# Thirty-six instead of thirty-two batches multiplied by the weight while x is first read, in a graph-layer kernel of Strassen products

## The reference, cut to what matters

```python
h = relu(layernorm(x))                  # x: 64 batches x 128 steps x 1024 nodes, float32
x_avg = mean of h over batches          # 1024 nodes x 128
sim = cosine similarity of the nodes    # 1024 x 1024, from x_avg
adj = (sim_score + gumbel0 > 1 - sim_score + gumbel1)
adj_sym = clip(adj + adj.T, 0, 1);  nmask = clip(adj_sym + eye, 0, 1)
common = nmask @ nmask.T
struct = where(adj_sym > 0 and common > 1, common / common.max() * common, 0)
W = adj * struct;  Wn = dinv[:, None] * W * dinv[None, :]
out = Wn.T applied to (h @ weight) over the nodes, for every batch, + bias
return x + out
```

## Time and profile before

| | |
|---|---|
| median of three runs | 921.62 us |
| the profiled execution, its own time | 921.26 us |
| its span | 919.5 us |
| TensorE busy | 887.7 us, 97% of the span |
| VectorE busy | 725.3 us, 79% |
| ScalarE busy | 328.0 us, 36% |
| GpSimd busy | 239.8 us, 26% |
| granted TensorE clock | 0.999 of full speed |

### The profile page before, as it was taken

The page is one execution under the profiler, slowest core; times in us unless marked ns, Lnnn a source line. Parts: engine busy times, 40 slices in busy tenths (PEclk is TensorE's granted clock), DMA queues, the critical chain, the costliest instruction groups (busy, mean ns, idle before and its releaser), DMA issues.

```text
span 919.5 us, 12305 instructions
## 1 busy us (share of the span) xinstructions
PE 887.7 (97%) x4563; PEld 761.4 (83%) x4567; DVE 725.3 (79%) x1471; ACT 328.0 (36%) x531; POOL 239.8 (26%) x188
## 2 busy tenths in 40 slices
PE   4999999999999999999999999999999999999997
PEld 3777665788788888888888888888889888988886
DVE  7878858899989797888879787868576758677687
ACT  4999935651221121302121211323333342424130
POOL 4799960500212121111111111302011111111111
PEclk9999999999999999999999999999999999999999
DMA  9999889233436170716344352615233252524122
GB/s 355 382 419 381 328 326 422 81 123 116 137 138 206 69 275 6 269 61 214 105 170 140 135 190 85 225 50 198 77 134 141 90 185 69 183 92 161 46 92 92
DMA packets 37484, 160.25 MB, mean 174 GB/s; under 512 B 3376, under 2 KB 3504, under 8 KB 32176
## 3 DMA queue, kind: packets, MB, share of 16 engines
q1 hardware_dynamic: 37424, 159.46, 46.8%
HBM read 108.07 MB, written 51.38 MB: 173 GB/s over the span
## 4 chain that ended last, share of the span: by engine, by line
PE 79%; DVE 9%; ACT 6%; POOL 3%; issue 2%; DMA 0%; DVEq 0%; ACTq 0%; POOLq 0%
PE ps L1354 69%; PE ps L1303 4%; ACT main L532 4%; DVE bmem L957 3%; POOL main L473 3%; ACT bmem L541 2%; PE ps L1224 2%; DVE stats L750 2%; PE ps L1206 1%; DVE bmem L950 1%; PE ps L1137 1%; PE ps L1284 1%; DVE main L1070 1%; DVE main L1046 1%; DVE bmem L969 0%
## 5 line engine op out<-in xcount | busy, mean ns | idle before, releaser
L1354 PE MATMUL ps<-bmem,main 128*128 128x256 f32 x3136 | 685.1, 379 | 4.0 <-DVE main L1037 2.6
L1354 PEld LDWEIGHTS ps<-bmem,main 128*128 128x128 f32 x3136 | 592.4, 190 | 83.3 <-DVE main L1037 3.5
L500 POOL TENSOR_TENSOR main<-main 128x256 f32<-128x256 f32 x32 | 28.7, 896 | 477.3 <-ACT main L659 424.0
L1037 DVE TENSOR_TENSOR main<-ps,main 128x512 f32<-128x512 f32 x124 | 76.5, 623 | 71.0 <-PE ps L1354 71.0
L490 POOL TENSOR_TENSOR main<-main 128x256 f32<-128x256 f32 (+1 forms) x96 | 91.9, 984 | 139.0 <-DVE main L1030 139.0
L1046 DVE TENSOR_TENSOR main<-main 128x256 f32<-128x256 f32 (+1 forms) x256 | 124.5, 558 | 0.0
L473 POOL TENSOR_TENSOR main<-main 128x1024 f32<-128x1024 f32 x41 | 96.9, 2364 | 23.4 <-ACT main L532 18.5
L619 ACT ACTIVATE ps<-ps 128x512 f32<-128x512 f32 x64 | 33.8, 528 | 159.2 <-PE ps L1354 159.2
L750 DVE BATCH_NORM_STATS2 stats<-main 128x6 f32<-128x512 f32 x128 | 81.2, 674 | 4.5 <-DMA main<-in_x 4.5
L877 DVE TENSOR_TENSOR main<-main 128x256 f32<-128x256 f32 x112 | 48.2, 431 | 44.7 <-PE ps L1354 41.5
L1137 PEld LDWEIGHTS ps<-w_sb,main 128*128 128x128 f32 x560 | 67.0, 194 | 15.0 <-issue 12.0
(11 more groups left out here) (101 smaller groups left out, 541.2 us busy)
## 6 DMA issues: line engine op xcount, KB each, us to landing
main<-in_x SPq DMA_DIRECT2D x92, 512.0 KB, 7.2
main<-in_x SPq DMA_DIRECT2D x32, 1024.0 KB, 6.7
out<-main SPq DMA_DIRECT2D x31, 1024.0 KB, 4.9
main<-spill SPq DMA_DIRECT2D x17, 1024.0 KB, 5.3
spill<-bmem SPq DMA_DIRECT2D x16, 1024.0 KB, 11.9
main<-in_L_gnn_gumbel SPq DMA_DIRECT2D x8, 1024.0 KB, 6.3
spill<-main SPq DMA_DIRECT2D x2, 512.0 KB, 4.6
out<-main SPq DMA_DIRECT2D x1, 512.0 KB, 4.9
```

What stands on the lines that cost most here:

```text
L1037: dve.tensor_tensor(at, piece(slot, b), at, ALU.add).then_inc(s, 1)
L1354: last = pe.matmul(piece(slot, b)[:, QUARTER * e:QUARTER * (e + 1)], left_[:, blk(c)], right_[:, c, :], start=slot in FRESH and b < 3 and ...
```

## The change

1. `SPILLED` gets two more pairs, 12 and 20: 18 pairs, 36 batches, are multiplied by the weight in stage 1. `LOADED` is then quads 2 to 10, `WEIGHED` quads 1 and 11 to 15, `EXTRA` is 11. Stage 3 multiplies four batches less.
2. `BOTH` has ten pairs in place of nine, other ones: GpSimd adds one batch more, TensorE one less.
3. The copies (5, 1), (9, 1), (13, 1) and (19, 1) are made by VectorE, before its last statistics instruction of groups 6, 8, 10 and 13. The other copies with b = 1 stand one step later in ScalarE's list: step p now makes the copy (p-4, 1) where it made (p-3, 1); the copy (p-2, 0) stays.
4. Six stores (twelve batches) stand between the reads of x in place of four, from p = 14 on.
5. Stage 2: of the first two transposed blocks, the parts that need only the first seven rows of `adj` stand ahead of the wait for the last.
6. The first quad of stage 3: slots 0, 2 and 6 issue first what needs only finished operands; VectorE adds up slot 4's results ahead of `prepare(6)` and makes the operands of quad 1's slot 0 earlier; `finish_kept(0, 1)` moves from quad 0 into quad 1.

```diff
-    SPILLED = [0, 1, 2, 3, 5, 7, 8, 9, 11, 13, 15, 17, 19, 21, 23, 26]
+    SPILLED = [0, 1, 2, 3, 5, 7, 8, 9, 11, 12, 13, 15, 17, 19, 20, 21, 23, 26]
-    SPILLED_EARLY = [15, 17, 19, 21]
-    HOMES = [*range(8, 16), *range(16, 24), *range(8), *range(8, 16)]
+    SPILLED_EARLY = [14, 16, 18, 20, 22, 24]
+    HOMES = [*range(8, 24), *range(8), *range(8, 20)]
+    BY_VECTOR = [5, 9, 13, 19]
+    LAG = (2, 4)
+    def product(p, b):
+        return 2 * SPILLED.index(p) + b
+    MADE = [product(q, b) for p in range(PAIRS) for q, b in ((p - 1, 1), (p, 0)) if q in SPILLED]
+    VECTOR_COPIES = [*(product(p, 1) for p in BY_VECTOR), KEPT - 2, KEPT - 1]
+    SCALAR_COPIES = [product(q, b) for p in range(PAIRS) for q, b in ((p - LAG[1], 1), (p - LAG[0], 0))
+                     if q in SPILLED and product(q, b) not in VECTOR_COPIES]
-    BOTH = [4, 6, 8, 11, 14, 16, 18, 20, 23]
+    BOTH = [4, 6, 8, 10, 12, 14, 16, 18, 20, 22]
+        def wait_copied(eng, n):
+            if n in VECTOR_COPIES:
+                eng.wait_ge(s_kept_vector, VECTOR_COPIES.index(n) + 1)
+            else:
+                eng.wait_ge(s_kept, SCALAR_COPIES.index(n) + 1)
+        def wait_made(eng, n):
+            eng.wait_ge(s_hw, MADE.index(n) + 1)
...
                 if p - HPAIRS in SPILLED:
-                    act.wait_ge(s_hw, 2 * SPILLED.index(p - HPAIRS) + 2)
+                    wait_made(act, product(p - HPAIRS, 1))
...
-                    if p - 3 in SPILLED[:-1]:
-                        keep(p - 3, 1)
-                    if p - 2 in SPILLED[:-1]:
-                        keep(p - 2, 0)
+                    for b in (1, 0):
+                        q = p - LAG[b]
+                        if q in SPILLED and product(q, b) in SCALAR_COPIES:
+                            keep(q, b)
...
+            def keep(p, b):
+                n = product(p, b)
+                wait_made(dve, n)
+                if HOMES[n] in HOMES[0:n]:
+                    dve.wait_ge(s_spill[HOMES.index(HOMES[n]) // 2], 16)
+                dve.tensor_copy(kept[:, HOMES[n], :], bank(2 + 2 * b, 2)).then_inc(s_kept_vector, 1)
...
                     long_step(t, 6)
+                    for p in BY_VECTOR:
+                        if t == (p + 7) // 2:
+                            keep(p, 1)
                     long_step(t, 7).then_inc(s_bn, 1)
...
             def keep_product(p, b):
-                n = 2 * SPILLED.index(p) + b
-                wait(pe, s_kept, n - 1)
+                n = product(p, b)
+                if n >= 2:
+                    wait_copied(pe, n - 2)
                 times_weight(h1[:, p % HPAIRS, b, :], 2 + 2 * b).then_inc(s_hw, 1)
...
-            transposes(0)
-            transposes(1)
+            for i in range(2):
+                for j in range(C - 1):
+                    transpose(i, j)
+            pe.wait_ge(s_adj, C)
+            for i in range(2):
+                transpose(i, C - 1).then_inc(s_tr, 1)
...
+                if quad == 1:
+                    inner_sums(quad, 3)
+                    finish_kept(0, 0, u_keep, s_g21, 0)
+                    finish_kept(0, 1, v_keep, s_g22, 8)
...
+                    if quad == 0 and slot in (0, 2, 6):
+                        if slot == 0:
+                            pe.wait_ge(s_comb, 4 * n + 4)
+                            pe.wait_ge(s_scaled, KC)
+                            pe.wait_ge(s_repc, 1)
+                            times(0, 0, 2, 0, q[0, 1], moving[1, 0])
+                            times(0, 0, 2, 1, s4, moving[1, 1])
+                            free(0, 0, 0)
+                            times(0, 0, 0, 0, q[0, 0], moving[0, 0])
+                            pe.wait_ge(s_repc, 2)
```

More of the change, by code:

```diff
@@ L338, in spill_group @@
             def spill_group(g):
[L339 to L342, removed]
+                wait_copied(sp, 2 * g)
+                wait_copied(sp, 2 * g + 1)
                 at = HOMES[2 * g]
@@ L678, in _ @@
                 for b in range(4):
-                    keep_bank(quad, 2, b, u_keep, 16 * quad, s_ukeep)
+                    keep_bank(quad, 2, b, u_keep, 8 if quad == 1 else 16 * quad, s_ukeep)
                     weigh(quad, (2, b))
                 for b in range(4):
-                    keep_bank(quad, 3, b, v_keep, 16 * quad - 8, s_vkeep)
+                    keep_bank(quad, 3, b, v_keep, 16 if quad == 1 else 16 * quad - 8, s_vkeep)
                     weigh(quad, (3, b))
@@ L768, in _ @@
                     for b in range(2):
[L769 to L772, removed]
+                        keep(SPILLED[-1], b)
                     whole_chain(t)
@@ L1008, in prepare @@
                     minus(rows_of(T4_ROWS), rows_of(B21_ROWS), rows_of(T2_ROWS), start)
+                    made_at["T4"] = made[0]
                     inner_of(6)
@@ L1094, in _ @@
                     inner_sums(quad, 2)
-                    finish_kept(quad - 1, 0, u_keep, s_g21, 16 * quad - 8)
                 else:
                     prepare(3)
-                if quad:
+                if quad == 1:
+                    inner_sums(quad, 3)
+                    finish_kept(0, 0, u_keep, s_g21, 0)
+                    finish_kept(0, 1, v_keep, s_g22, 8)
+                elif quad:
+                    finish_kept(quad - 1, 0, u_keep, s_g21, 16 * quad - 8)
                     inner_sums(quad, 3)
@@ L1109, in _ @@
                 if quad == 0:
+                    add_kept(quad, 4, v_keep, s_vkeep, s_g22)
                     prepare(6)
@@ L1113, in _ @@
                     finish_kept(quad, 0, u_keep, s_ukeep, 16 * quad)
-                add_kept(quad, 4, v_keep, s_vkeep, s_g22)
+                if quad:
+                    add_kept(quad, 4, v_keep, s_vkeep, s_g22)
                 if quad + 1 < QUADS:
@@ L1117, in _ @@
                 if quad == 0:
-                    finish(quad, 1)
-                    add_kept(quad, 6, u_keep, s_ukeep, s_g21, range(2))
-                finish_kept(quad, 1, v_keep, s_g22, 16 * quad + (0 if quad + 1 < QUADS else 8))
-                if quad:
-                    finish(quad, 1)
+                    add_kept(quad, 6, u_keep, s_ukeep, s_g21, range(1))
+                else:
+                    finish_kept(quad, 1, v_keep, s_g22, 16 * quad + (0 if quad + 1 < QUADS else 8))
+                finish(quad, 1)
                 if quad + 1 < QUADS:
-                    add_kept(quad, 6, u_keep, s_ukeep, s_g21, range(4) if quad else range(2, 4))
+                    add_kept(quad, 6, u_keep, s_ukeep, s_g21, range(4) if quad else range(1, 4))
                     dve.wait_ge(s_g21, 4 * quad + 4)
@@ L1209, in _, with transpose @@
             late_half(3, 1).then_inc(s_late_hw, 1)
-            pe.wait_ge(s_adj, C)
+            pe.wait_ge(s_adj, C - 1)
+            def transpose(i, j):
+                return pe.transpose(ps[:, 4 + i % 2, :].bitcast(BF16)[:, blk(j)], adj[:, j, blk(i)], identb[:, :])
             def transposes(i):
-                if i >= 2:
-                    pe.wait_ge(s_sym, i - 1)
+                pe.wait_ge(s_sym, i - 1)
                 for j in range(C):
-                    last = pe.transpose(ps[:, 4 + i % 2, :].bitcast(BF16)[:, blk(j)], adj[:, j, blk(i)], identb[:, :])
+                    last = transpose(i, j)
                 last.then_inc(s_tr, 1)
```

48 lines of the change are left out of this document (28 added, 20 removed).

## The result

The changed kernel takes 957.29 us (median of 4 runs, 956.19 to 958.29), the kernel before 922.25 (4 runs, 921.16 to 922.99): a ratio of 1.0381, 95% interval 1.0361 to 1.0400. It is slower by 35 us. The forecast was 937.2 us and its range ended at 942: the sign and the place were right, the size was less than half of what came.

The account below looks back on a forecast made before the run. TensorE was taken to bound stage 3 and ScalarE stage 1. Stage 1 +26.5, stage 3 -7.1, first quad and transposes -3.5 gave +15.9 on 921.26: 937.2 us, range 926 to 942.

Parts of the forecast that it names:

- the chunks': Stage 3: eight chunks of matmuls fewer, 0.89 us each on the chain; gain 7.1 us.
- the order of waits: Stage 1, the deciding term: later ScalarE copies with b = 1 make engines wait; stage 1's end +26.5 us.
- The ring: Inside one ScalarE step of stage 1, copy, product, product, copy wait in turn; 4.85 us where ScalarE needs 0.90.
- The count by engine: Stage 1: each engine's added work, leaving out who waits for whom; growth of 1.6 to 5.4 us.
- (a): GpSimd's adds keep the end of stage 1; only the extra add shows, +1.6 us, 912.3 us in all; chance 0.08.
- (b): TensorE sets the pace of stage 1; +5.4 us, 916.1 us in all; chance 0.05.
- (c): Stage 1: only the full rings cost, +12.4 to +19 us, 923 to 930 us in all; chance 0.10.
- Rival (d): Stage 1: VectorE waits for products, so statistics are late; another 5 to 10 us, 942 to 947 us; chance 0.07.
- the three handoffs: Stage 1: copy to waiting product 1.08 us, product to next product 1.79, product to waiting copy 1.98; sum 4.85.
- full gap: ScalarE's wait in stage 1 between copies (p-4, 1) and (p-2, 0); forecast 3.95 us, four times.
- half gap: ScalarE's wait in stage 1 between copy (p-4, 1) and relu(p+1); forecast 2.16 us, four times.
- the walk: Step-by-step count of stage 1's in-order lists and measured handoffs; its end at 149.7, +26.5 us; chance 0.70.

Follow-up runs that it names:

- experiment 1: Changed kernel with ScalarE's copies with b = 1 back at step p-3 (LAG = (2, 3)); 916.02 us, ratio 0.9935.
- Experiment 8: experiment 5 with `finish_kept(0, 1)` moved behind the operands of slot 4 in quad 1; 912.46 us, ratio 0.9900.
- experiment 5: experiment 1 with, in quad 1, `finish_kept(0, 0)` ahead of slot 3's operands and `finish_kept(0, 1)` behind `finish(1, 0)`; 913.82 us, ratio 0.9907.
- 6: Experiment 3 with quad 1's VectorE order as in experiment 5; 920.53 us, ratio 0.998.
- Experiment 2: Changed kernel with 12 or 19 unused 128x128 products ahead of each of the eight products that close a ring; 943.93 us, ratio 1.0243.
- experiment 7: experiment 1 with VectorE's four copies back on ScalarE (`BY_VECTOR` empty); 918.06 us, ratio 0.9951.
- Experiment 3: Changed kernel with stage 1's lists as before (32 batches) and LAG = (2, 3), only transposes and quads changed; 922.26 us, ratio 0.9999.
- experiment 4: Experiment 3 with ScalarE's copies with b = 1 one step later (LAG = (2, 4)); 944.31 us, ratio 1.0244.

## Why the prediction was wrong in size and right in mechanism

**The ledger in spans.** Forecast: +26.5 - 7.1 - 3.5 = +15.9. Measured: stage 1 +40.8, its end +2.5, transposes and quad 0 -3.7, quad 1 +4.5 (experiment 1 against 8), and with the chunks' -7.1 (experiment 5 against 6) that is +37.0 of the +37.1.

**Right: the order of waits.** The ring is there, in the steps that were named, and it alone costs (experiment 1). The count by engine, which the prediction worked out and then did not believe (+1.6 to +5.4 us), came out as +1.8 once the ring was opened: the count is good as long as nobody waits, and says nothing of a ring. Rivals (a), (b) and (c) are out, for the gaps are all there and larger. Rival (d) had VectorE's statistics late behind its copies. Its 942 to 947 us come nearest of all, but its mechanism is not what happened: ScalarE's waits for VectorE in stage 1 after 20 us are 1.2 + 0.2 us.

**The step that failed: the price of the three handoffs.** The prediction took 1.79 us for a product and 1.98 from a product's start to the copy behind it, both from the earlier trace rows, where TensorE had idled 1.25 us or less and ran at 1.00. No sentence of it asked for the clock behind the waits that it forecast, so the lower level stood in the sum at nothing, without a reason. The first handoff holds, 27.96 to 29.02 is 1.06 (1.08). From the product at 29.02 to the copy at 34.52 it is 5.50, where 1.79 + 1.98 = 3.77 were taken. In starts, a full gap is 34.52 - 27.96 = 6.56 three times (44.46 and 75.51 alike) and 99.48 - 94.54 = 4.94 once, against 4.85; a half gap is 52.67 - 47.64 = 5.03 three times and 4.40 once, against 1.08 + 1.98 = 3.06.

- full gaps: 3 x 6.56 + 4.94 - 4 x 4.85 = +5.2 us
- half gaps: 3 x 5.03 + 4.40 - 4 x 3.06 = +7.3 us
- small waits, step 23 and what else the rows leave over: 14.3 - 12.5 = +1.8 us, not taken apart

Together they are the 14.3 us by which stage 1 (164.05 - 149.7) was missed. Experiment 2 takes the clock's share away and leaves 151.40 - 149.7 = 1.7 of it. So 12.65 of the 14.3 us (164.05 - 151.40) hang on the clock, and the walk's own logic was off by 1.7 us over 27 us.

The Trainium skill (TensorE: Matmul & The Clock Gate, Part 1: The HAM clock gate) says that the halved rate is TensorE's default state and that activity releases the full one, with nothing in between; the rows show these two levels (0.50 at 30 to 32 us, 1.00 at 34 to 36). The same page (Why this matters for your kernels) advises against idle gaps between bursts of matmuls, above a length that it names. The rule spoke against this change and was not weighed. Taken by its length alone it would still have missed the turns at 38.95 and 70.01 us, where the clock fell behind gaps of 2.75 us, which are shorter; the rows decide. A forecast of waits on TensorE has to ask what its first work behind each wait costs at the lower level: here 3.55 us (48.79 to 52.34) for one product that takes 1.79, and 5.47 for two that take 3.73.

**Not foreseen: the end of stage 1, +2.5 us.** "It moves as a block" supposed that VectorE's L853 is the last thing to be late. With the ring TensorE is late too, and its column sums come 3.95 us behind L853 in place of 1.4. In experiment 1 the same L857 follows L853 without that wait (125.01 to 128.49); in experiment 7 it waits 1.16 us. From L853 to the first matmul of stage 3 the distance is 229.00 - 164.05 = 64.95 us against 187.55 - 123.21 = 64.34 before, within the 1 us that the forecast allowed; that is luck, since the 2.5 us are offset by the wait of 1.39 us that is gone and by smaller gains.

**Right: the first quad.** TensorE's idle time there goes from 1.39 + 0.48 + 1.76 + 0.89 = 4.5 us to 0.61 + 0.49 = 1.1: 3.4 us. The transposes give 0.3. Forecast 3.5, measured 3.7. The row that the prediction held against this part did not decide it: the eight moved sums and the eight beside them take 7.05 us together in quad 1, 0.44 each, though the operands L908, L911 and L914 took 0.95, 0.94 and 0.83 us from 274.30 on, beside GpSimd's adds.

**Wrong: the quad that receives `finish_kept`.** The prediction found 42.00 - 34.69 = 7.3 us of VectorE free there and cost the move at nothing. Free time on average is not free time at the place: the piece of 7.05 us stands ahead of `finish(1, 0)`. Experiment 8, which differs from experiment 1 in the places of this piece's two halves alone, is shorter by 915.1 - 910.6 = 4.5 us. Of these 2.5 are the wait, and most of the rest is the clock behind it. In medians it is 916.02 - 912.46 = 3.6: two of experiment 1's four executions had spans of 913.4 and 913.5 and a clock of 0.999, where the profiled one had 0.997. In experiment 2 the same wait of 2.48 us was not followed by a lower clock, and the stretch from its end to the end of the span took 942.2 - 286.24 = 655.96 us there, against 956.6 - 298.92 = 657.68 in the changed kernel: 1.7 us is the clock's share. Experiment 3 shows the balance, 3.7 won and some 4.5 lost, and no change in the time that can be measured. So the forecast's -3.5 for the order of the first quads was right for quad 0 and came to nothing as a whole.

**Right: stage 3.** L1345 has 384 records, and experiments 5 and 6 differ by 7.1 us from quad 1 on, for 36 batches against 32.

**What stays open.** Which idle stretches lower the clock can't be told from these runs: 2.75 us did at 36 to 39 us and did not at 93 to 96, and some 2.5 us in quad 1 did in the changed kernel and did not in experiment 2. Even one kernel differs: of experiment 3's ten executions eight had a span of 920.4 us or more and a mean clock of 0.997 or less, and two had 918.9 and 0.999. That these two are the ones without the fall in quad 1 fits the 1.7 us, but was not seen in a profile, and the kernel before, which has no such wait in quad 1, falls into two groups as well: beside experiment 3, six of its thirteen executions had a span of 920.0 us or less and seven 921.1 or more, with a clock of 0.997 or less. In experiment 4 a wait of 2.75 us at 73 us was not followed by a fall, and the first full gap came to 6.59 us. A forecast can only hold both ends.

## What to carry to other kernels

When two in-order engines hand buffers to each other, write down for each instruction who frees its buffer, and follow the chain until it comes back to the same engine. If it returns inside one step, every handoff is paid at each turn, and no count of busy time shows it. Price each handoff with the durations that TensorE has after an idle stretch of that length, not with those from a stretch in which it never idled; keep both as ends of the range. And before a piece of work is put where an engine is free on average, look at what stands right behind it in that engine's list and who waits for that.

## What the runs showed of the hardware

Unexpected was that the lower clock hit nearly every turn of the ring. TensorE's idle stretches of 2.75 to 4.37 us were followed by the 1.2 GHz level in seven of the eight turns of rings, while from 23 to 123 us it was busy for 73.76 of 100 us. Filling these stretches with 124 matmuls of 128x128 of no use won 14.4 us of span (956.6 - 942.2). One product (16 records) right behind a stretch of 4.37 us took some 3.6 us, where it takes 1.79 otherwise. Two in a row behind one of 2.75 us or 3.34 us took 5.47 together, where they take 3.73. So one turn at the lower level cost some 1.7 to 1.8 us in either case. The clock had not yet fallen when the two at 29.02 began: seven records start from 28 to 30 us, where it was 0.95, and eleven from 30 to 32, where it was 0.50.
